# Rounded copies of queries and keys for the maxima scores of the differential attention stage

## The reference

```python
Q = (X @ W_q).reshape(b, n, H, 2 * DH).transpose(0, 2, 1, 3)      # H = 8, DH = 16
K = (X @ W_k).reshape(b, n, H, 2 * DH).transpose(0, 2, 1, 3)
Q1, Q2 = (Q[..., :DH], Q[..., DH:])
K1, K2 = (K[..., :DH], K[..., DH:])
A1 = jnp.where(causal, jnp.einsum('bhqd,bhkd->bhqk', Q1, K1) * scaling, neg_inf)
A2 = jnp.where(causal, jnp.einsum('bhqd,bhkd->bhqk', Q2, K2) * scaling, neg_inf)
attn = jax.nn.softmax(A1, axis=-1) - lam * jax.nn.softmax(A2, axis=-1)
O = jnp.einsum('bhqk,bhkd->bhqd', attn, V)
```

## Time and profile before

| | us |
|---|---|
| median of 3 runs | 2727.38 |
| lowest and highest | 2725.24, 2733.45 |
| the profiled execution | 2741.41 |
| its span, first to last instruction | 2739.7 |

### The profile page before, as it was taken

One profiled execution on the slowest core, in us unless ns is written; L12 is line 12 of the kernel. 1 busy time (PEld: TensorE's weight loads), 2 busy tenths in 40 slices (PEclk: granted clock), 3 DMA queues, 4 the chain that ended last, 5 costly groups with the idle time before them and its releaser, 6 DMA issues. The chain is left out here.

```text
span 2739.7 us, 62417 instructions
## 1 busy us (share of the span) xinstructions
PE 2291.8 (84%) x19720; PEld 1664.5 (61%) x19720; DVE 1782.2 (65%) x4946; ACT 1581.4 (58%) x3505; POOL 1285.7 (47%) x2450
## 2 busy tenths in 40 slices
PE   5999997899698887997888887888576788888786
PEld 3666665699465555896755555587233455555685
DVE  5667766444577874444767786466777578886555
ACT  3555554467476663675668787334355378876233
POOL 3557665355257775253234555364300334554463
PEclk9999998899799998998989998899777989998998
DMA  8000000322200003123000000224000000001124
GB/s 317 3 5 13 12 13 11 93 66 69 66 2 14 15 17 95 42 71 91 4 1 7 15 17 26 67 73 111 11 0 6 4 1 10 15 17 60 44 73 129
DMA packets 133614, 116.66 MB, mean 43 GB/s; under 512 B 22903, under 2 KB 119685, under 8 KB 131264
## 3 DMA queue, kind: packets, MB, share of 16 engines
q1 hardware_dynamic: 116032, 78.17, 9.8%
q0 software_dynamic: 17280, 34.65, 3.9%
HBM read 58.22 MB, written 56.36 MB: 42 GB/s over the span
## 5 line engine op out<-in xcount | busy, mean ns | idle before, releaser
L1188 ACT ACTIVATE A_Pm<-A_t 128x768 f32<-128x768 f32 (+1 forms) x512 | 469.2, 916 | 206.7 <-PE A_t L1611 203.2
L340 POOL DMA_INDIRECT ybuf<-F_yo,F_idx x284 | 315.3, 1110 | 330.2 <-issue 147.6
L1603 PE MATMUL A_s<-A_K,A_Q 32*128 32x256 f32 (+1 forms) x2640 | 326.8, 340 | 75.9 <-DVE A_mx L1391 48.8
L1391 DVE TENSOR_REDUCE A_mx<-A_s 128x4 f32<-128x1024 f32 x264 | 321.6, 1218 | 84.9 <-PE A_s L1603 79.3
L1070 POOL TENSOR_SCALAR_AFFINE_SELECT A_Pm<-A_Pm 128x256 f32<-128x256 f32 x512 | 218.3, 450 | 225.2 <-ACT A_Pm L1188 223.5
L1638 PE MATMUL A_ot<-A_Pm,A_V 128*32 128x256 f32 (+3 forms) x3640 | 300.7, 395 | 27.2 <-POOL A_Pm L1070 19.6
L192 POOL DMA_INDIRECT xbuf<-xs,dst x256 | 260.3, 1017 | 129.9 <-issue 63.5
L691 PE MATMUL F_hb<-F_xT,F_wt 128*128 128x128 f32 x2272 | 311.8, 281 | 3.1 <-DVE F_wt L549 1.5
L1603 PEld LDWEIGHTS A_s<-A_K,A_Q 32*128 32x128 f32 x2640 | 194.2, 188 | 192.2 <-DVE A_mx L1391 95.7
L1611 PE MATMUL A_t<-A_Q,A_K 32*128 32x256 f32 (+1 forms) x2560 | 306.6, 333 | 0.0
L691 PEld LDWEIGHTS F_hb<-F_xT,F_wt 128*128 128x128 f32 x2272 | 281.3, 195 | 12.0 <-issue 5.5
(11 more groups left out here) (436 smaller groups left out, 5086.3 us busy)
## 6 DMA issues: line engine op xcount, KB each, us to landing
F_xr<-xbuf SPq DMA_DIRECT2D x284, 68.0 KB
xbuf<-A_zero SPq DMA_DIRECT2D x16, 1088.0 KB, 17.4
xs<-ybuf SPq DMA_DIRECT2D x32, 512.0 KB, 6.9
ybuf<-F_yo,F_idx POOLq DMA_INDIRECT x284
xbuf<-xs,dst POOLq DMA_INDIRECT x256
F_WA<-in_L_ffn_ew SPq DMA_DIRECT2D x2, 2048.0 KB
F_WA<-in_L_ffn_ew SPq DMA_DIRECT2D x16, 256.0 KB
F_WA<-in_L_ffn_e_gate SPq DMA_DIRECT2D x2, 1024.0 KB
```

The lines of the kernel that those rows point to most:

```text
L340: pool.indirect_dma_start(out=YBUF[:, :], out_offset=bass.IndirectOffsetOnAxis(ap=idx[n][:, h:h + 1], axis=0), in_=yo[r][:, h, :], in_offs ...
L1188: act.activation(Pm[r][:, j:j + 2, :], tbank[:, :].rearrange("p (j k) -> p j k", j=2)[:, :, 0:PW], ACT.Exp, scale=SCALE).then_inc(t_free, 1)
L1391: last = dve.reduce_max(tops.rearrange("p t j -> p j t"), sbank[:, :].rearrange("p (j t k) -> p j t k", j=2, t=TPS), AX)
L1603: last = pe.matmul(sbank[:, k * 512 + o:k * 512 + o + nk], Q1[q][r, c + t * P:c + (t + 1) * P], K1[q][r, c:c + nk], start=not masked, stop ...
```

## The change

`Qr` and `Kr` are new float32r tiles of the same shape as Q1 and K1, two of each. In `quads`, ahead of the take, ScalarE writes one of them from the same PSUM bank, without the bias that K1 gets. `score` reads Qr and Kr in place of Q1 and K1, in this stage only. `score_t` and `with_max` still read the float32 tiles.

```diff
+    if diff:
+        Qr, Kr = [[sb(f"{n}r_{k}", [P, NTL * SEQ], F32R) for k in range(2)] for n in "QK"]
+    QS, KS = (Qr, Kr) if diff else (Q1, K1)
...
             def quads(m, k, q, misc):
                 c = slice(k // 2 * 512, (k // 2 + 1) * 512)
+                if diff:
+                    act.wait_ge(misc_full, m + 1)
+                    act.activation((Kr if k % 2 else Qr)[q][:, c], misc[:, :], ACT.Identity)
                 if k % 2:
                     take(m, K1[q][:, c], misc[:, :], bias=colc[:, :])
...
-                    last = pe.matmul(sbank[:, k * 512 + o:k * 512 + o + nk], Q1[q][r, c + t * P:c + (t + 1) * P], K1[q][r, c:c + nk],
+                    last = pe.matmul(sbank[:, k * 512 + o:k * 512 + o + nk], QS[q][r, c + t * P:c + (t + 1) * P], KS[q][r, c:c + nk],
```

## The result

| | before | after |
|---|---|---|
| median of 16 runs each, us | 2727.64 | 2720.76 |
| lowest and highest | 2717.44, 2737.09 | 2709.33, 2730.08 |
| ratio after / before | | 0.9971, 95% interval 0.9957 to 0.9985 |

The change makes the kernel 0.3% faster: by the ratio about 7.9 us, between 4 and 12, and the interval leaves out no change at all. The prediction was 2722.5 us with a gain of 4.9. The two profiled executions differ by more, 2741.41 against 2717.41 us, but single executions of one kernel lie 20 us apart; what can be compared in them is the stage, where the steps of two executions of the changed kernel agree to a hundredth of a us.

What follows compares the result with a forecast made beforehand. TensorE was taken to bound the stage A1, busy 77.74 of 80.00 us. The terms 0 - 1.3 - 3.6 + 0 = -4.9 us took the median 2727.4 to 2722.5 us; range 2710 to 2740.

Steps and rivals of the forecast that it cites:

- The half quad, 0.00: In each of 128 groups on TensorE, transposed scores stay float32 and end as before, so 0.00 us changes.
- Rival A: In the half quads: strips share something, passes cost in sum, so groups shorten; 24 us, about 2698; chance 10%.
- C: In the half quads: float32 and float32r do not run side by side; up to +0.43 each, 2782; chance 6%.
- The lead-in, -1.3: In the four groups without transposed scores, three get 0.43 us shorter each: -1.3 us.
- The one wait, -3.6: TensorE's wait for GpSimd's mask in quad 2: 0.32 less in ten sequences, 3.2 us, and 0.4 in the others.
- The copies, 0: 69 copies from PSUM on ScalarE, 0.60 us each, 41 us of work, lie beside TensorE and cost 0.
- rival B: In quad 1 copies delay the exponential and GpSimd's first mask: slower, 2736, or 2768 if every quad pays; chance 13%.
- the signs named ahead: Half quads 0.86, score rows 1056 to 528, VectorE's maximum at 0.53, mask wait 8.3 us, ScalarE +41, no new ScalarE wait.
- Rival D: Whole kernel: the earlier sum does not reach TensorE and the lead-in gives nothing; 2727 us; chance 11%.

Runs made afterwards that it cites:

- the mirror: Against the changed kernel, maxima scores read float32 and transposed scores read the rounded keys and a float32r Q2: 2719.74 us, one run.
- maxima-first kernel: Changed kernel with both maxima scores issued ahead of both transposed ones: 2720.38 us, ratio 0.9962; a second one also has the lead-in in float32: ratio 0.9968.
- the copies alone: Changed kernel with the rounded copies written, but maxima scores still reading the float32 tiles: 2727.33 us against 2726.69 before, ratio 0.9995.
- The second copy: Changed kernel with ScalarE writing each bank once more into a spare tile, 69 more copies: 2733.12 us, one run, against 2744.93 before.

## Why the prediction was right, and what was off

The mechanism was right: the half quad keeps its length, the gain is in the lead-in and in one wait, and the copies are free. That the sum came within 1 us of the stage's 5.7 is partly luck, since one term was mis-sized in two places that offset each other and two small gains were not in the sum.

- *The half quad, 0.00.* Right but for 7 ns: 0.8 us over the stage. The step-by-step reading of the transposed scores held. Rivals A and C are gone: the half quad did not shorten, and float32r and float32 passes run side by side. The run with both scores rounded and the mirror show that the longer pair sets the length. Rival A even took the saving too small. With both scores rounded, a transposed score of 256 columns is followed by the next one after 0.22 us (206.88 to 207.10), of which 0.10 is the load: about 0.12 by this estimate, against two passes of 0.22 in float32. So about three quarters of the maxima scores' columns went, and still the half quad is only 7 ns shorter.
- *The lead-in, -1.3.* Measured -1.30 in the profile of the change and in its repetition.
- *The one wait, -3.6.* Measured -3.0. The mechanism was right and the size of its first link wrong: VectorE starts 0.20 earlier and not 0.44. In the ten sequences that were to gain 0.32 each, 3.2 us, the wait fell by 0.18 each, 1.8 us. In the other six, which were to gain 0.4 us together, it fell by 0.19 each, 1.2 us. There the prediction had the copy hold the exponential back by 0.16. In sequence 7 it starts 236.85 - 235.72 = 1.13 after its group before and 233.24 - 232.06 = 1.18 after:

```profile
235.72 0.38 PE L1603 MATMUL A_s<-A_K,A_Q 32*128 32x128 f32 x2
```

```profile
232.06 0.33 PE L1609 MATMUL A_s<-A_Kr,A_Qr 32*128 32x128 f32 x2
...
232.63 0.71 ACT L1235 ACTIVATE xs<-A_rxn 128x256 f32<-128x256 f32 x2
...
233.24 0.80 ACT L1194 ACTIVATE A_Pm<-A_t 128x768 f32<-128x768 f32 x1
```

- *The reason for the 0.20* was at hand. The Trainium skill ("TensorE: Matmul & The Clock Gate", Part 3, The mechanism) has matmuls start and end in program order; I set it aside, since the starts in the earlier trace rows do not keep it. The starts do not, in the maxima-first kernel even less: the transposed scores start at 207.28 and the maxima scores that stand ahead of them in the program at 207.43. But the signals do: VectorE's start moved with the order in the program and nothing else in the maxima-first kernel, and the exponential of the mirror was held by passes that it does not read. The prediction gave 0.21 for VectorE by that rule, and 0.20 was measured. The wait's term was then -2.5 and the sum -3.8; the measured 3.0 is 0.5 above it, with 1.2 in place of 0.4 in the six sequences and 1.8 in place of 2.1 in the ten.
- *The copies, 0.* Right, by the copies alone: 0.9995. The second copy shows that the margin was real and small, and rival B's mechanism true of a ScalarE with one more copy. Of the signs named ahead, ScalarE's busy time was off with VectorE's start: 29.6 us more and not 41. The rows of the maxima scores fell from 1056 to 528 as said. The one new wait of TensorE for ScalarE is of 0.3 us, once, in the lead-in.
- *What I did not have.* The exponential also starts 0.05 earlier, which is worth 0.56 us behind the turned routing input, and the groups' 0.8. Together these 1.4 us are more than the 0.6 that the wait's term lacked: 1.3 + 3.0 + 0.8 + 0.56 = 5.7 against 4.9. The first group also starts 0.3 to 0.5 us earlier in the two profiles of the change than in that of before; with the copies alone it does not, with one more copy it starts 0.2 earlier. I cannot say what it hangs on.
- *Rival D, nothing changes,* falls with the interval of the ratio and with the 6.1 us of the stage. The whole time gives 7.9 us, 4 to 12. The stage gives 5.7 to 6.1. The remaining 2 us are inside the interval; no run tells whether they exist.

## What to carry to other kernels

Passes saved on one side of the array are worth nothing when the matmuls on the other strips take as long (0.859 against 0.866 us here): follow each strip's own chain of starts, and ask which one the next stage of work waits for. To shorten such a group, both sides have to shrink (0.43). In these traces a matmul's signal came only after the matmuls ahead of it in the program, also those on other strips, so the one that another engine needs first is to be issued first (0.54 in place of 0.77 us).

## What the runs showed of the hardware that was not expected

- Signals in program order across strips: the one-pass scores of the mirror, whose last pass ends at about +0.45 of a group of 0.85 us, release their reader no sooner than two-pass ones (1.01 against 1.03 us).
- Two ScalarE copies from one PSUM bank follow each other at 0.49 us, each 0.60 long.
- Starts across strips, against it, can leave the program's order: in the maxima-first kernels a transposed score starts at +0.01 of its group and the maxima score ahead of it in the program at +0.16.
- TensorE's granted clock can come in full in the lead-in, at 28.5 to 28.8 us, and fall to 0.50 at about 35.5 for 3 to 14 us. It did so in three executions of four, with TensorE busy for 4.70, 4.88 and 5.30 of the 7.00 us before; in the fourth it was busy for 5.21 and the clock stayed. It costs a lead-in 1.4 to 1.8 us and, in the maxima-first kernel, 3 us in the first quads of the stretch (410.54 against 407.53 without).
